# K and V projection of a transformer layer: 256 normalised tokens at a time against 512 raw tokens with centred weights

## The reference, cut to what matters

```python
def _layernorm(x, axis=-1, eps=1e-5):
    m = jnp.mean(x, axis=axis, keepdims=True)
    v = jnp.var(x, axis=axis, keepdims=True)
    return (x - m) / jnp.sqrt(v + eps)
...
    q = (x @ wq + bq).reshape(B, S, H, D)
    k = (x @ wk + bk).reshape(B, S, HKV, D)
    v = (x @ wv + bv).reshape(B, S, HKV, D)
...
    x = x + _L0_attn_ref(_layernorm(x, axis=-1), ...)
    x = x + _L0_ffn_ref(_layernorm(x, axis=-1), ...)
```

## Time and profile before

| | before |
|---|---|
| median of 3 runs (lowest to highest) | 2751.34 us (2750.67 to 2753.62) |
| profiled execution, its own time | 2754.83 us |
| its span on the slowest core, 0 | 2753.3 us |
| the cores' spans | 2740.9 to 2753.3 us |
| TensorE busy | 2475.3 us (90%) |
| VectorE, ScalarE, GpSimd busy | 933.6, 611.1, 76.4 us |
| mean granted TensorE clock, core 0 | 0.956 |

### The profile page before, as it was taken

The page is one execution under the profiler, slowest core; times in us unless marked ns, Lnnn a source line. Parts: engine busy times, 40 slices in busy tenths (PEclk is TensorE's granted clock), DMA queues, the critical chain, the costliest instruction groups (busy, mean ns, idle before and its releaser), DMA issues.

```text
span 2753.3 us, 33937 instructions; the slowest of 8 cores (2740.9 to 2753.3 us)
## 1 busy us (share of the span) xinstructions
PE 2475.3 (90%) x12258; PEld 1144.6 (42%) x12258; DVE 933.6 (34%) x1660; ACT 611.1 (22%) x732; POOL 76.4 (3%) x148
## 2 busy tenths in 40 slices
PE   4787878368888888899999999999999999999999
PEld 2454545123333333344444444444444444444444
DVE  2333333435455554134333333321123333333201
ACT  1111111226666666232011111100001111111000
POOL 0000000000000000000000000000000000000000
PEclk7888888679999999899999999999999999999999
DMA  8221212010010034750433333367733333332763
GB/s 149 37 43 35 46 31 47 15 31 16 16 24 16 16 54 77 177 141 12 87 62 63 57 57 71 68 131 160 176 71 73 73 73 73 64 62 47 165 158 95
DMA packets 50897, 197.67 MB, mean 72 GB/s; under 512 B 7057, under 2 KB 7442, under 8 KB 40498
## 3 DMA queue, kind: packets, MB, share of 16 engines
q0 software_dynamic: 20736, 144.19, 29.7%
q1 hardware_dynamic: 30002, 51.31, 5.9%
HBM read 314.48 MB, written 25.17 MB: 123 GB/s over the span
## 4 chain that ended last, share of the span: by engine, by line
PE 82%; DVE 6%; ACT 5%; DMA 3%; issue 3%; DVEq 0%; ACTq 0%; SPq 0%; POOLq 0%
PE pq L1170 28%; PE pq L1332 14%; PE pq L420 4%; PE pq L429 4%; PE pq L541 4%; PE pq L1197 4%; PE pq L1182 4%; PE pq L1248 3%; PE pq L797 3%; PE pq L635 3%; PE pq L683 3%; PE pq L381 2%; ACT wa_sq L355 2%; ACT wc_p L648 2%; PE pq L699 1%
## 5 line engine op out<-in xcount | busy, mean ns | idle before, releaser
L1170 PE MATMUL pq<-dv_xln,dw_wsl 128*128 128x512 bf16 x3584 | 810.1, 379 | 0.1
L1170 PEld LDWEIGHTS pq<-dv_xln,dw_wsl 128*128 128x128 bf16 x3584 | 350.1, 98 | 424.4 <-issue 3.5
L1332 PE MATMUL pq<-dx_x2s,dw_wsl 128*128 128x512 bf16 x1792 | 390.4, 379 | 1.7 <-DVE ds_x L1232 1.4
L648 ACT ACTIVATE wc_p<-pq,gl_nb 128x1024 bf16<-128x1024 f32 (+4 forms) x288 | 293.2, 1041 | 132.9 <-PE pq L635 126.5
L1232 DVE TENSOR_TENSOR ds_x<-ds_s,pq 128x512 bf16<-128x512 bf16 x108 | 74.3, 688 | 645.4 <-PE pq L1197 634.1
L1215 ACT ACTIVATE ds_s<-pq 128x512 bf16<-128x512 f32 x112 | 66.9, 597 | 938.8 <-PE pq L1197 920.5
L1332 PEld LDWEIGHTS pq<-dx_x2s,dw_wsl 128*128 128x128 bf16 x1792 | 175.0, 98 | 214.2 <-issue 3.9
L683 PE MATMUL pq<-wc_p,pp_V 128*128 128x512 bf16 (+3 forms) x576 | 163.9, 367 | 19.4 <-DVE wc_p L659 12.9
L541 PE MATMUL pq<-pp_xlnown,wc_wq 128*128 128x512 bf16 x512 | 147.0, 393 | 8.8 <-DMA wc_wq<-wq_h 5.9
L1350 DVE TENSOR_TENSOR dx_stg<-pq,dx_stg 128x512 f32<-128x512 f32 x64 | 41.6, 687 | 331.2 <-PE pq L1332 163.2
L1182 PE MATMUL pq<-dp_c,dw_wsl 128*128 128x512 bf16 x448 | 133.2, 379 | 1.7 <-DVE dp_d L994 1.7
(11 more groups left out here) (158 smaller groups left out, 1989.7 us busy)
## 6 DMA issues: line engine op xcount, KB each, us to landing
dw_wsl<-w_h POOLq DMA_DIRECT2D x56, 1216.0 KB, 9.3
wa_xb<-x_tiles POOLq DMA_DIRECT2D x16, 1024.0 KB, 10.1
dw_wsl<-w2b_h POOLq DMA_DIRECT2D x16, 960.0 KB, 9.8
dw_wsl<-w2a_h POOLq DMA_DIRECT2D x16, 896.0 KB, 8.3
dw_ev<-xo_oc SPq DMA_DIRECT2D x32, 256.0 KB, 4.6
wc_wq<-wq_h POOLq DMA_DIRECT2D x16, 512.0 KB, 5.3
wo_w<-wo_h POOLq DMA_DIRECT2D x16, 512.0 KB, 14.2
xres_d<-dw_ev SPq DMA_DIRECT2D x32, 256.0 KB, 3.0
```

Source lines behind the costliest of these rows:

```text
L648: lambda e: e.activation(out=ps[:, lo:hi], in_=b_s[r][:, lo:hi], func=AF.Exp, bias=nb[h % 2]),
L1170: ms = [(lambda hc, bank=bank, wo_=wo_: (lambda e: e.matmul(bank[:, 0:TD], w[:, wo_ + hc * 128: wo_ + (hc + 1) * 128], xln2[tt][:, hc * TD ...
L1332: ms.append((lambda j=j, t=t: (lambda e: e.matmul(banks[t][:, 0:TD], w[:, j * 128:(j + 1) * 128], x2s[:, j * 2 * TD + t * TD: j * 2 * TD + ...
```

## The change

Keys and values are now computed from raw (bf16, not normalised) tokens in 8 groups of 512. With column-centred weights, W minus the mean of each column, x·W needs no mean of x, and the factor 1/std of each token is applied to the result: for K along the free dimension by a VectorE multiplication in place in PSUM, followed by ScalarE adding the bias and writing K (`k_out`); for V, where tokens lie on partitions, as a scalar for each partition (`v_mm`). That scalar comes from `rtok`, a [128, 4] tile that SyncE fills by writing the row of 1/std to DRAM and reading it back transposed (`moments`).

The weights are centred on the chip (`centre`: 16 matmuls with ones, four VectorE operations of 128x2048, for each of W_k and W_v). The sums of group j+1 stand between the four V parts of group j, and are made with 32 columns of ones, four at a time in different column quarters of the array. Groups 0 and 1 are the own tokens; they are loaded straight into `xlnown`, and normalised there by `own_ln` after their K and V are done, so `xo_tiles` and its four tiles are gone. Groups 2 to 7 go through three buffers `xr`. The squares and norms of K are taken in each group (`k_norm`). The weights of query heads 0 and 1 are loaded after group 5. The eight `q` groups of heads 0 and 1 are put in another order, with four different PSUM banks, and `q_norm(1, 1)`, `q_bound(1)` and `q_select(1)` go into the attention of head 0. The first loads of `xo_oc` move from the start to head 12.

```diff
-TA = 256
-NTA = S // TA
-NTB = TOWN // TA
-NT = NTA + NTB
+CK = 512
+NCK = S // CK
...
-    x_tiles = din('x_tiles', [NTA, 128, NCH * TA])
-    xo_tiles = din('xo_tiles', [NTB, 128, NCH * TA])
+    x_tiles = din('x_tiles', [NCK, 128, NCH * CK])
...
+        xr = [WA.al(f'xr{i}', [128, NCH * CK], BF16) for i in range(3)]
+        sqr = [WA.al(f'sqr{i}', [128, 4 * CK], BF16) for i in range(2)]
...
-        for dst, src in ((ocb_sb, c_ocb), (ocf_sb, c_ocf), (orf_sb, c_orf)):
+        for dst, src in ((onb_sb, c_onb), (ocf_sb, c_ocf), (wgt_sb, wgt_h)):
...
+        for dst, src in ((selm_sb, c_selm), (selq_sb, c_selq), (bk_sb, bk_h), (bvr_sb, bv_h),
+                         (onf_sb, c_onf), (sel4_sb, c_sel4), (idb_sb, c_idb),
+                         (sel8_sb, c_sel8), (exps_sb, c_exp), (tri_sb, c_tri), (lab_sb, c_lab),
+                         (lsel_sb, lsel_h), (vsel_sb, vsel_h), (bq_sb, bq_h), (bo_sb, bo_h)):
+            d_consts = P.dma('sync', dst, src, sem='dCon')
...
+        def x_view(j):
+            if j < 2:
+                return xlnown.rearrange('p (c n) -> p c n', c=NCH)[:, :, j * CK:(j + 1) * CK]
+            return xr[(j - 2) % 3].rearrange('p (c n) -> p c n', c=NCH)
+        def load_x(j):
+            src = x_tiles[j].rearrange('p (c n) -> p c n', c=NCH)
+            if j < 2:
+                x_tok[j] = [(f'dX{j}{p}', P.dma('gpsimd', x_view(j)[:, 4 * p:4 * p + 4, :],
+                                                src[:, 4 * p:4 * p + 4, :], sem=f'dX{j}{p}')) for p in range(4)]
+                return
+            if j >= 5:
+                P.wait('gpsimd', 'pe', v_pe[j - 3])
+            x_tok[j] = [(f'dXr{(j - 2) % 3}', P.dma('gpsimd', x_view(j), src, sem=f'dXr{(j - 2) % 3}'))] * 4
+        def load_w(dst, src, tag):
+            return [(f'd{tag}{p}', P.dma('gpsimd', dst[:, p * 2048:(p + 1) * 2048],
+                                         src[:, p * 2048:(p + 1) * 2048], sem=f'd{tag}{p}')) for p in range(4)]
+        def centre(w, toks, bank, key, free=()):
+            for p in range(4):
+                pe = P.g('tensor', [(lambda hc: (lambda e: e.matmul(
+                    bank[:, 0:512], onb_sb, w[:, hc * 512:(hc + 1) * 512],
+                    start=(hc == 0), stop=(hc == NCH - 1), skip_group_check=True)))(hc)
+                    for hc in range(4 * p, 4 * p + 4)], waits=[toks[p], ('dC1', d_c1), *free], inc='pe')
+            for p in range(4):
+                wv3 = w[:, p * 2048:(p + 1) * 2048].rearrange('p (c n) -> p c n', c=4)
+                ctr_ve[(key, p)] = P.g('vector', [(lambda wv3: (lambda e: e.scalar_tensor_tensor(
+                    wv3, bank[:, 0:512].rearrange('p (o n) -> p o n', o=1).to_broadcast([128, 4, 512]),
+                    -1.0 / HID, wv3, op0=ALU.mult, op1=ALU.add)))(wv3)], waits=[('pe', pe)], inc='ve')
...
+        def sums(j, p):
+            n, s = sq_tok[(j, p)]
+            buf = sqr[n % 2]
+            ms = []
+            for r in range(2):
+                for g in range(4):
+                    i = 2 * r + g % 2
+                    mov = x_view(j)[:, 4 * p + i, :] if g < 2 else buf[:, i * CK:(i + 1) * CK]
+                    ms.append((lambda r, g, mov: (lambda e: e.matmul(
+                        st_b[32 * g:32 * g + 32, 0:CK], onb_sb[:, 0:32], mov,
+                        start=(p == 0 and r == 0), stop=(p == 3 and r == 1), skip_group_check=True)))(r, g, mov))
...
+            s1_pe[j] = sq_user[n] = P.g('tensor', ms, waits=wts, inc='pe')
+        def moments(j):
+            rs = rs_t[j % 2]
+            v = P.g('vector', [lambda e: e.tensor_copy(stA, st_b[:, 0:CK])], waits=[('pe', s1_pe[j])], inc='ve')
+            pe = P.g('tensor', [
+                lambda e: e.matmul(mn_b[:, 0:CK], selm_sb, stA, start=True, stop=True, skip_group_check=True),
+                lambda e: e.matmul(st_b[:, 0:CK], selq_sb, stA, start=True, stop=True, skip_group_check=True),
+            ], waits=[('ve', v), ('ve', kr_ve[j - 1]) if j else ('dCon', d_consts)], inc='pe')
...
+            s = P.g('scalar', [lambda e: e.activation(out=rs, in_=mn_b[:, 0:CK], func=AF.Square)],
+                    waits=wts, inc='sc')
+            v = P.g('vector', [lambda e: e.scalar_tensor_tensor(
+                rs, st_b[:, 0:CK], EPS, rs, op0=ALU.add, op1=ALU.subtract)], waits=[('sc', s)], inc='ve')
+            s = P.g('scalar', [lambda e: e.activation(out=rs, in_=rs, func=AF.Ln)], waits=[('ve', v)], inc='sc')
+            rs_sc[j] = P.g('scalar', [lambda e: e.activation(out=rs, in_=rs, func=AF.Exp, scale=-0.5)],
+                           waits=[('sc', s)], inc='sc')
...
+            P.wait('sync', 'sc', rs_sc[j])
+            row_st[j] = P.dma('sync', rst_d[j:j + 1, :], rs[0:1, :], sem=f'tS{j % 2}')
+            P.wait('sync', f'tS{j % 2}', row_st[j])
+            if j >= 2:
+                P.wait('sync', 've', vev_ve[(j - 2, 3)])
+            tok_ld[j] = P.dma('sync', rtok[j % 2], rst_d[j].rearrange('(t p) -> p t', p=128),
+                              sem=f'tL{j % 2}', slow=True)
...
+        def k_mm(j, kv, lo=0, hi=NCH):
...
+            return P.g('tensor', [(lambda hc: (lambda e: e.matmul(
+                c_k[kv][:, 0:CK], wk_sb[:, hc * 512 + kv * 128: hc * 512 + (kv + 1) * 128],
+                x_view(j)[:, hc, :], start=(hc == 0), stop=(hc == NCH - 1), skip_group_check=True)))(hc)
+                for hc in range(lo, hi)], waits=wts, inc='pe')
+        def k_out(j, kv, pe):
+            kv_ve[(j, kv)] = P.g('vector', [
+                lambda e: e.tensor_mul(c_k[kv][:, 0:CK], c_k[kv][:, 0:CK], rs_t[j % 2]),
+            ], waits=[('pe', pe), ('sc', rs_sc[j])], inc='ve')
+            ks = K_sb[:, kv * S + j * CK: kv * S + (j + 1) * CK]
+            kb_sc[(j, kv)] = P.g('scalar', [
+                lambda e: e.activation(out=ks, in_=c_k[kv][:, 0:CK], func=AF.Identity, bias=bk_sb[:, kv:kv + 1]),
+            ], waits=[('ve', kv_ve[(j, kv)]), ('dCon', d_consts)], inc='sc')
...
+            sq_tok[('k', j)] = P.g('scalar', [
+                lambda e: e.activation(out=buf[:, kv * CK:(kv + 1) * CK], in_=ks, func=AF.Square),
+            ], waits=[('sc', kb_sc[(j, kv)])] + wts, inc='sc')
+        def k_norm(j):
+            n, buf, _ = ksq_use[j]
...
+            sq_user[n] = P.g('tensor', [(lambda kv: (lambda e: e.matmul(
+                mn_b[32 * kv:32 * kv + 32, 0:CK], onb_sb[:, 0:32], buf[:, kv * CK:(kv + 1) * CK],
+                start=True, stop=True, skip_group_check=True)))(kv) for kv in range(NKV)], waits=wts, inc='pe')
+            kr_ve[j] = P.g('vector', [lambda e: e.reduce_max(kmx[:, j:j + 1], mn_b[:, 0:CK], axis=AXX)],
+                           waits=[('pe', sq_user[n])], inc='ve')
+        def v_mm(j, sub):
...
+            v_pe[j] = P.g('tensor', [(lambda hc: (lambda e: e.matmul(
+                c_v[sub % 2][:, 0:512], x_view(j)[:, hc, sub * 128:(sub + 1) * 128],
+                wv_sb[:, hc * 512:(hc + 1) * 512],
+                start=(hc == 0), stop=(hc == NCH - 1), skip_group_check=True)))(hc)
+                for hc in range(NCH)], waits=wts, inc='pe')
+            ci = j * 4 + sub
+            vev_ve[(j, sub)] = P.g('vector', [lambda e: e.scalar_tensor_tensor(
+                V_sb[:, ci * 512:(ci + 1) * 512], c_v[sub % 2][:, 0:512], rtok[j % 2][:, sub:sub + 1], bvr_sb,
+                op0=ALU.mult, op1=ALU.add)],
+                waits=[('pe', v_pe[j]), (f'tL{j % 2}', tok_ld[j]), ('dCon', d_consts)], inc='ve')
+        def own_ln(j, p):
+            xv = x_view(j)[:, 4 * p:4 * p + 4, :]
...
+            v = P.g('vector', [lambda e: e.tensor_mul(xv, xv, bc(rbA[j][:, 0:CK]))],
+                    waits=[('pe', v_pe[j]), ('ve', ap_ve[(j, 'rb')])], inc='ve')
+            ap_ve[j] = P.g('vector', [lambda e: e.tensor_add(xv, xv, bc(rbA[j][:, CK:2 * CK]))],
+                           waits=[('ve', v)], inc='ve')
+        wk_tok = load_w(wk_sb, wk_h, 'K')
+        load_x(0)
+        wv_tok = load_w(wv_sb, wv_h, 'V')
+        for j in range(1, 5):
+            load_x(j)
+        centre(wk_sb, wk_tok, c_v[0], 'k')
...
+        for p in range(4):
+            squares(0, p)
+            kpe = [k_mm(0, kv, 4 * p, 4 * p + 4) for kv in range(NKV)]
+            sums(0, p)
+        moments(0)
+        for kv in range(NKV):
+            k_out(0, kv, kpe[kv])
+        centre(wv_sb, wv_tok, c_v[1], 'v', [('ve', sw_ve)])
+        k_norm(0)
+        for j in range(NCK):
+            nxt = j + 1 < NCK
+            if j:
+                kpe = []
                 for kv in range(NKV):
...
+                    kpe.append(k_mm(j, kv))
+                    if kv == 0:
+                        moments(j)
+                    if kv == 1 and nxt:
+                        squares(j + 1, 0)
+                    if kv >= 1:
+                        k_out(j, kv - 1, kpe[kv - 1])
+                    if j <= 2:
+                        own_ln(j - 1, kv)
+                k_out(j, NKV - 1, kpe[NKV - 1])
+            elif nxt:
+                squares(1, 0)
```

(34 more changed lines are left out.)

344 lines of the change are left out of this document (102 added, 242 removed).

## The result

| | before | after |
|---|---|---|
| median of 4 (lowest to highest) | 2752.3 us (2750.7 to 2753.6) | 2505.6 us (2504.1 to 2660.6) |
| profiled execution, its span | 2754.8, 2753.3 us | 2506.8, 2505.3 us (core 5; the cores 2494.5 to 2505.3) |
| ratio, 95% interval | | 0.9102, 0.9084 to 0.9120 |
| TensorE busy, mean granted clock | 2475.3 us, 0.956 | 2356.3 us, 0.984 |

Faster by 247 us. 2481 was forecast; the time is 24.6 us above that, inside the range of 2462 to 2508, near its upper end.

A forecast was written before the change was run, and what follows sets the result against it. Ahead of the first scores, the order of waits, not a busy engine, was taken to set 27.2 us a tile. Cutting 601.4 to 331.5 us saves 270, from the median 2751.34 to 2481; range 2462 to 2508.

The forecast's parts named there:

- main case: Whole kernel: the forecast without any rival, 2481 us, own range 2466 to 2494, given a 60% chance.
- rivals 1 and 2: Start of the kernel: late constants (2500 us, 14%) and slow small pieces of x (2485 to 2508 us, 14%).
- a small delay in each group: Every group: the rtok load outlasting its cover by 3 us, counted into the range's upper end of 2508.
- The start, to V(0): Group 0: K starts at 22.5 us; TensorE waits for W_v's centring, done at 61 us.
- V(0), the step that failed: Group 0's V with sums: 3 us for the low clock plus 16.6, from 61 to 81 us.
- the rule: rtok load: 33 packets on each DMA engine, each behind a 16 KB row of 1.5 us.
- Group 1: 37.7 us, to 119, including some 5 us where V part 2 waits for rtok behind large rows.
- Groups 2 to 6: Five whole groups of 32.7 us each, 163.5 us together, with TensorE busy all through.
- Behind the first scores: Everything after the first scores: 2151.9 us, taken as unchanged.
- Rival 1: Start: constants land late and delay group 0's moments; 19 us more, 2500 us; 14%.
- Rival 2: Groups 0 and 1: loads of x in small pieces run slower or hold the queue; 2485 to 2508 us; 14%.
- Rival 3: Every group: single-element load slow by itself; 3 us beyond cover gives 2505 us, 6%; losing the whole gain, 1%.

The follow-up runs named there:

- e5: e1 with group 0's first V part in four pieces, each behind its quarter of W_v's centring, and k_norm(0) moved behind it; 2476.2 us.
- e6: e1 without the centring of W_v (V lacks the mean term) and with k_norm(0) behind the first V part; 2476.8 us.
- e7: e1 with the four parts of the next group's sums behind the four V parts instead of between them; 2520.3 us.
- e1: The changed kernel with the loads of groups 2 to 4 issued only after group 0's rtok has landed; 2477.5 us.
- e9: The changed kernel with groups 2 to 4 loaded in eight pieces (2 KB rows) from the start, plus e5's quarters; 2474.6 us.
- e2: The changed kernel with groups 2 to 4 each loaded in four pieces (4 KB rows), same order and place; 2477.5 us.
- e3: The changed kernel with groups 2 to 4 each loaded in two pieces (8 KB rows), same order and place; 2494.2 us.
- e8: e1 with six extra single-element loads, one after the other, ahead of each group's rtok load on SyncE's queue; 2551.5 us.

## Why the prediction was right, and where it was not

Of the 270 us, 247 came. The mechanism of the gain was right: whole groups at 32.2 us with TensorE never waiting. That 2505.6 lies in the range is luck: it is 12 us outside the main case's own 2466 to 2494, and the range reached 2508 for rivals 1 and 2 and a small delay in each group, none of which happened. In the traces the first scores start at 353.2 and not 331.5. The 21.7 us by steps:

- **The start, to V(0).** K(0) at 25.5 (22.5 forecast), moments at 44.7 released by VectorE's copy, V(0) at 62.05 (61 forecast): 1 us. The centring operation took 2.22 us, 2.4 estimated, and made up for a part of the late start.
- **V(0), the step that failed.** "V(0) with its sums ends at 61 + 3 + 16.6 = 81"; it ended at 110.2 and took 48.1 us instead of 20. The prediction had the rule (33 packets, each behind a 16 KB row) and applied it to group 1's load, at 92, only. Group 0's is asked for at 54.7, 17 us before V part 2 wants it, and groups 2 to 4 came in until 101. By the same rule it lasts nearly as long as the large rows do: 26.9 us of waiting, and 2.5 for the second fall to the low clock (6.03 against 3.5). Applied with the prediction's own 108 us for the last large row (100.9 measured), the rule would have given a wait of some 36 us (an estimate) and a time above the range.
- **Group 1**: 37.7 forecast, 34.3 measured. Its 5 us stall did not come, since by then no large rows were left; 2.1 us of waiting for a square did. e5 and e6 show the stall, 3.9 and 3.4 us, where group 0 is as fast as forecast. The square that TensorE waits for starts at 133.37, right behind ScalarE's last K result, and ahead of each of the last three K results ScalarE waits 1.6 us for VectorE's multiplication. That `own_ln` on VectorE is what spaces these was argued and not tried.
- **Groups 2 to 6**: 5 x 32.17 against 5 x 32.7, **group 7** 29.8 against 30.1, **heads 0 and 1** 18.1 against 18.6: 3.5 us less in sum; with 1 + 28.1 - 3.4 that is 22.2, and the 0.5 left is rounding in the prediction's own chain. A part of sums costs what was forecast: V parts start 4.09 us apart (160.04 to 164.13), of which 16 matmuls are 3.45: 0.64. The half microsecond a group comes from the matmuls, 10.36 us for 48 and so 0.216 each, not 0.219, and from k_norm, which adds 0.24 between 164.13 and 168.46, not 0.4.
- **Behind the first scores**: 2152.1 against 2151.9. Most of the 2.9 us left to the median come from the profiled executions, 3.5 us above their median before and 1.2 after.

Rival 1 (late constants) is out: the moments of group 0 were released by VectorE. The selection matrices landed 12 and 15 us after their issue. The trace also settles the doubt about packets: queue 0's 23808 are, with 136 other transfers of 128 + 16, eight of 512 + 16, so each 1 KB row was a packet. The Trainium skill ("DMA: Bandwidth & Descriptors", the section on SWDGE vs HWDGE vs iDMA) says that a DMA engine changes over only between packets and that one is preferably at most 4096 bytes. The counts here show 8 and 16 KB rows, above that size, as one packet each, and the landings with 4, 8 and 16 KB rows are what such a packet costs the queue beside it. Rival 2 (small pieces) is out: x group 0, in pieces, landed at 37.5 (36 forecast) and group 1 at 64.3 (66), and K(0) waited for none of them. Rival 3 in its small form (2505) gives the measured time, but by the wrong mechanism: it had 3 us in each of 8 groups, and the runs show one delay of 27 in one group. Rival 4 did not happen, and e7 shows at what placing it would.

## What to carry to other kernels

A small transfer of many elements costs, on a busy DMA engine, its packets times the time of a row of whatever large transfer is under way; check every such transfer against the large ones issued before it, the first above all. The one that stalled here (asked for at 54.7) came before the one that the prediction had checked (at 92). Large transfers that nobody needs yet are better cut in short rows or held back than left whole. And a gain at one wait counts only as far as the next wait: remove one and look at what stands 30 us behind it.

## What the runs showed of the hardware

- The same 512 single elements, asked for at 54 to 58 us, landed after 5.2 to 7.6 us where rows of 1 KB alone were coming in (e1), 12.0 to 14.7 where rows of 2 KB followed these (e9), 18.5 to 19.6 with 4 KB (e2), 29.6 to 31.3 with 8 KB (e3), 42.8 to 43.9 with 16 KB (the change), and 2.0 with nothing beside it. In the change 528 packets of 4 bytes and 547 rows (374 of 16 KB, 173 of 1 KB) started in the same stretch. Even the 2 KB store ahead of it took 5.0 us (49.68 to 54.67) to be waited for, against 1.25 (118.54 to 119.79) with nothing beside it.
- `selq` landed after 15 us at a start with rows of 1 and 4 KB on queue 0, and after 35.6 with rows of 8 and 16 KB; the constants ahead of it differ too, so this is no clean comparison.
- After waits of 3.4, 3.9 and 7.7 us (e6, e5, e8) TensorE ran its next 16 matmuls in 5.6, 5.8 and 5.3 us instead of 3.6; after one of 1.7 us (e9) it did not. A wait of 2.1 us for a square in group 1 went either way: in e2 the granted clock was then 0.50 (110 to 112) and the 16 matmuls took 5.31 us, in the change it stayed at 1.00 (136 to 140) and they took 3.63.
